# Renumbering the places of all pieces in a planned decoder layer, with own places for the first and the last batch

## The reference

```python
# part 1: attention against a fixed memory of 1024 rows, 4 heads of 64 channels
x = _layernorm(residual, ln_g, ln_b)
scores = jnp.einsum('bhtd,sd->bhts', q, k)
p = jnp.square(jax.nn.relu(scores))
out = jnp.einsum('bhts,sd->bhtd', p, v)          # residual + out
# part 2: cross attention, 16 heads of 16 channels
logits = jnp.einsum('bhqd,bhkd->bhqk', Q, K) * scale
D = jnp.clip(frac[:, None, :] - frac[:, :, None], CLAMP_MIN, CLAMP_MAX)
stoich_bias = ap * jnp.maximum(D, 0.0)[:, None] + an * jnp.minimum(D, 0.0)[:, None]
probs = jax.nn.softmax(gamma * logits + delta * stoich_bias, axis=-1)
# part 3: eight experts with a common matrix and a LoRA of rank 4 each; the gate's argmax picks one
lora = jnp.einsum('bsr,fr->bsf', jnp.einsum('bsd,rd->bsr', x, lora_A[i]), lora_B[i])
inter = jax.nn.relu(base + lora)
expert_out = jnp.einsum('bsf,df->bsd', inter, wo_W) + wo_b
# the layer
x = _layernorm(x + attn(x)); x = _layernorm(x + xattn(x, ctx)); x = _layernorm(x + ffn(x))
```

## Time and profile before

| | |
|---|---|
| median of 3 runs | 916.64 us (914.18 to 917.05) |
| profiled execution, device time | 914.81 us |
| its span in the profile | 913.0 us |
| mean granted PE clock | 0.992 of full speed |
| instructions | 20283 |
| PE busy | 857.1 us, 94% |
| DVE busy | 778.7 us, 85% |
| ACT busy | 690.3 us, 76% |
| POOL busy | 533.2 us, 58% |
| DMA | 46.10 MB, mean 50 GB/s |

### The profile page before, as it was taken

One profiled execution on the slowest core, in us unless ns is written; L12 is line 12 of the kernel. 1 busy time (PEld: TensorE's weight loads), 2 busy tenths in 40 slices (PEclk: granted clock), 3 DMA queues, 4 the chain that ended last, 5 costly groups with the idle time before them and its releaser, 6 DMA issues.

```text
span 913.0 us, 20283 instructions
## 1 busy us (share of the span) xinstructions
PE 857.1 (94%) x7140; PEld 682.6 (75%) x7140; DVE 778.7 (85%) x2286; ACT 690.3 (76%) x1453; POOL 533.2 (58%) x620
## 2 busy tenths in 40 slices
PE   2697989999999999999999999999999999999876
PEld 1344767878878787877887787887878787788666
DVE  3869989889998998989898998989899897899842
ACT  3557889788787878878787978878797887877721
POOL 2757776666656765666666666665666565533210
PEclk9989999999999999999999999999999999999998
DMA  5223322222122223122222322212222312223000
GB/s 151 87 46 68 65 47 54 36 54 41 35 48 58 54 48 64 35 44 55 39 54 58 54 44 53 45 32 51 59 54 47 64 33 32 58 38 66 14 13 23
DMA packets 40022, 46.10 MB, mean 50 GB/s; under 512 B 10257, under 2 KB 27153, under 8 KB 39922
## 3 DMA queue, kind: packets, MB, share of 16 engines
q1 hardware_dynamic: 39922, 44.82, 24.6%
HBM read 15.42 MB, written 4.19 MB: 21 GB/s over the span
## 4 chain that ended last, share of the span: by engine, by line
PE 83%; DVE 8%; ACT 3%; issue 2%; DMA 1%; POOL 1%; SPq 0%; POOLq 0%; DVEq 0%
PE bank L218 28%; PE bank L262 12%; PE bank L343 11%; PE bank L250 7%; PE bank L334 6%; PE bank L355 6%; PE bank L251 6%; PE bank L282 2%; PE bank L404 2%; DVE bank L761 2%; PE bank L365 1%; DVE T L768 1%; DVE R L717 1%; DMA STG<-in_WvT 1%; PE bank L239 1%
## 5 line engine op out<-in xcount | busy, mean ns | idle before, releaser
L964 POOL TENSOR_SCALAR U<-DP,alph 128x512 f32<-128x512 f32 x256 | 181.5, 711 | 153.6 <-DVE NM L768 92.3
L953 POOL TENSOR_TENSOR R<-R 128x512 f32<-128x512 f32 x212 | 221.9, 1052 | 78.4 <-ACT R L496 78.4
L548 ACT ACTIVATE P<-T,NM 128x256 f32<-128x256 f32 x512 | 232.0, 508 | 3.2 <-DVE NM L768 2.7
L761 DVE SCALAR_TENSOR_TENSOR bank<-DN,alph,bank 128x512 f32<-128x512 f32 x256 | 191.9, 750 | 36.7 <-PE bank L334 35.0
L475 ACT ACTIVATE STG<-bank 128x512 f32<-128x512 f32 x256 | 152.5, 596 | 70.5 <-PE bank L343 69.1
L768 DVE CUSTOM_DVE_ANT_0 T<-bank,U 128x256 f32<-128x256 f32 x512 | 197.0, 422 | 8.8
L496 ACT ACTIVATE R<-bank 128x512 f32<-128x512 f32 x256 | 151.8, 597 | 54.4 <-PE bank L251 53.3
L343 PE MATMUL bank<-ident,P 128*128 128x128 f32 x1024 | 154.6, 273 | 5.0 <-ACT STG L475 4.8
L343 PEld LDWEIGHTS bank<-ident,P 128*128 128x128 f32 x1024 | 119.3, 140 | 24.0 <-ACT P L548 8.4
L262 PE MATMUL bank<-R,VS 128*32 128x512 f32 x1024 | 124.5, 604 | 5.5 <-DVE R L717 5.2
L250 PE MATMUL bank<-SK,KH 128*128 128x512 f32 x256 | 114.9, 449 | 8.2 <-DVE SK L711 7.6
(11 more groups left out here) (165 smaller groups left out, 1863.3 us busy)
## 6 DMA issues: line engine op xcount, KB each, us to landing
QS<-QK SPq DMA_DIRECT2D x384, 64.0 KB, 2.3
XG<-in_x SPq DMA_DIRECT2D x16, 256.0 KB, 2.7
CT<-in_ctxT SPq DMA_DIRECT2D x16, 256.0 KB, 3.6
out<-XO SPq DMA_DIRECT2D x16, 256.0 KB, 2.2
FK<-in_frac SPq DMA_DIRECT2D x16, 128.0 KB, 3.5
STG<-in_wiT SPq DMA_DIRECT2D x2, 512.0 KB, 3.5
STG<-in_woT SPq DMA_DIRECT2D x2, 512.0 KB, 4.0
STG<-in_kT SPq DMA_DIRECT2D x2, 256.0 KB, 4.0
```

The source lines that it names most:

```text
L548: eng.activation(P[n % NP][:, cs], T[n % NT][:, cs], ACT.Exp, bias=NM[:, n % 8, q:q + 1], scale=-1.0).then_inc(s_ex, 1)
L761: eng.scalar_tensor_tensor(out=L[:, :], in0=dn[:, :], scalar=alph[:, 16 + h:17 + h], in1=L[:, :], op0=ALU.mult, op1=ALU.add).then_inc(s_t1, 1)
L953: eng.tensor_tensor(r[:, :], r[:, :], r[:, :], ALU.mult).then_inc(s_sqp, 1)
L964: eng.tensor_scalar(U[n % NU][:, :], dp[:, :], alph[:, h:h + 1], 0.0, ALU.mult, ALU.add).then_inc(s_u, 1)
```

## The change

Every piece stays, with the same instructions. `due` gets two more arguments: `early` is added to the place of batch 0, `late` to that of batch 15 (batches 1 to 14 keep the common place). Nearly every place gets a new number, and so do the places of the pieces that come once (the weights, the staged loads, the constants, the memsets). As places fix nothing but the order of a queue, what changes is that order: 161 of PE's 1313 pieces, 220 of ACT's 1083, 203 of DVE's 698, 210 of POOL's 584 and 85 of SP's 140 stand at another position of their queue.

```diff
-        def due(g, first, count=1, step=0, start=0):
+        def due(g, first, count=1, step=0, start=0, early=0, late=0):
             for u in range(count):
-                b, over = divmod(g - first - step * u, PERIOD)
-                if over == 0 and start <= b < NB:
+                at = g - first - step * u
+                if at == early and start == 0:
+                    yield 0, u
+                b, over = divmod(at, PERIOD)
+                if over == 0 and max(start, 1) <= b < NB - 1:
                     yield b, u
+                if at == PERIOD * (NB - 1) + late:
+                    yield NB - 1, u
...
@@ PE
-                for b, u in due(g, 1322, 4, 24):
+                for b, u in due(g, 1323, 4, 25, early=1, late=292):
                     ffn_in(b, u)
...
-                for b, u in due(g, -939, 4, 141):
+                for b, u in due(g, -939, 4, 141, early=34):
                     av(b, u)
...
-                for b, _ in due(g, 1265):
+                for b, _ in due(g, 1269, early=-4, late=255):
                     uT(b)
-                for b, u in due(g, -1159, 16, 37):
+                for b, u in due(g, -1159, 16, 37, early=8):
                     scores(b, u)
-                for b, _ in due(g, -1219):
+                for b, _ in due(g, -1226, early=-87, late=9):
                     xnT(b)
...
@@ ACT
-                if g == -740:
+                if g == -577:
                     weight("i0", WI[0][:, 0:1, :], view(1024, 0, 128, 1))
...
-                if g == -853:
+                if g == -718:
                     weight("p0", WP[0][:, 0:4, :], view(1024, 1, 128, 4))
-                if g == -847:
+                if g == -665:
                     weight("p1", WP[0][:, 4:8, :], view(1024, 2, 128, 4))
...
-                for b, _ in due(g, 1282):
+                for b, _ in due(g, 1269, early=-17, late=303):
                     ulh(b)
...
@@ DVE
-                for b, _ in due(g, 2):
+                for b, _ in due(g, 1, early=-11, late=8):
                     differences(b)
...
-                for b, u in due(g, 14, 16, 39):
+                for b, u in due(g, 12, 16, 39, early=2, late=-2):
                     biased(16 * b + u)
...
-                if g == -1944:
+                if g == -2010:
                     dve.wait_ge(d_x[0], 16)
                     stats("a", 0, XG[0])
-                for b, _ in due(g, -1422):
+                for b, _ in due(g, -1428, early=-272, late=-4):
                     dve.wait_ge(s_xnT, b)
                     centred("a", b, XN, XG[b % 2], s_x0)
-                if g == -1392:
+                if g == -1513:
                     first_gain()
-                for b, _ in due(g, -1499, start=1):
+                for b, _ in due(g, -1491, start=1, late=-3):
...
-                for b, _ in due(g, 866):
+                for b, _ in due(g, 885, early=-23, late=-8):
                     low("aoT", b, CL, CH, s_aoh, s_aol)
-                for b, _ in due(g, -1215):
+                for b, _ in due(g, -1218, early=-178):
                     skl(b)
...
-                for b, _ in due(g, 2064):
+                for b, _ in due(g, 2020, early=-28, late=338):
                     dve.wait_ge(d_o, 16 * b)
                     centred("d", b, XO, X2b, s_xo)
-                if g == -629:
+                if g == -825:
                     dve.wait_ge(d_small, 160)
                     eng.tensor_scalar(bqk[:, 0:2], bqk[:, 0:2], gd[:, 0:1], 0.25, ALU.mult, ALU.mult)
                     eng.tensor_scalar(alph[:, :], alph[:, :], gd[:, 1:2], None, ALU.mult).then_inc(s_small, 1)
-                if g == -1825:
+                if g == -1430:
                     weight("v", W["v"][1][:, :, :], view(512, 1, 128, 2), W["v"][0][:, :, :])
-                if g == -1328:
+                if g == -1203:
                     weight("k", W["k"][1][:, :, :], view(512, 2, 128, 2), W["k"][0][:, :, :])
...
-                if g == -528:
+                if g == -479:
                     weight("i0", WI[1][:, 0:1, :], view(1024, 0, 128, 1), WI[0][:, 0:1, :])
-                if g == -967:
+                if g == -859:
                     weight("i1", WI[1][:, 1:2, :], view(1024, 2, 128, 1), WI[0][:, 1:2, :])
-                if g == -642:
+                if g == -596:
                     weight("p0", WP[1][:, 0:4, :], view(1024, 1, 128, 4), WP[0][:, 0:4, :])
-                if g == -536:
+                if g == -482:
                     weight("p1", WP[1][:, 4:8, :], view(1024, 2, 128, 4), WP[0][:, 4:8, :])
-                if g == 74:
+                if g == -17:
                     weight("g", GA[1][:, :, :], view(80, 0, 128, 2), GA[0][:, :, :])
-                if g == -82:
+                if g == -191:
                     weight("lb", LB[64:96, :], stage(1024, 2)[64:96, :], LB[64:96, :])
...
-                for b, _ in due(g, 1278):
+                for b, _ in due(g, 1283, early=-15, late=249):
                     ull(b)
-                for b, u in due(g, -1147, 16, 39):
+                for b, u in due(g, -1140, 16, 38, early=24, late=-10):
                     if on_dve(b, u):
                         square(b, u)
...
@@ POOL
-                for b, _ in due(g, -1305, start=1):
+                for b, _ in due(g, -1326, start=1, late=4):
                     gain(b)
...
-                for b, u in due(g, -1085, 16, 36):
+                for b, u in due(g, -1087, 16, 36, early=36, late=7):
                     if not on_dve(b, u):
                         square(b, u)
...
@@ SP
-                for b, u in due(g, 78, 4, 119):
+                for b, u in due(g, 109, 4, 119, early=1, late=-121):
                     restack(4 * b + u)
-                for b, _ in due(g, 85, start=1):
+                for b, _ in due(g, -235, start=1, late=-196):
                     load_f(b)
```

More of the change, by code:

```diff
@@ L440, in _ @@
                     values(4 * b + u)
-                for b, _ in due(g, -410):
+                for b, _ in due(g, -428, early=17, late=-22):
                     otT(b)
-                for b, _ in due(g, 885):
+                for b, _ in due(g, 894, early=-5, late=5):
                     turned_over("aoT", b, AO, s_ao, 2 * b + 2, s_aoT)
-                for b, _ in due(g, 925):
+                for b, _ in due(g, 924, early=-4, late=-2):
                     op(b)
-                if g == -1022:
+                if g == -1051:
@@ L448, in _ @@
                     bias_o()
-                for b, _ in due(g, -262):
+                for b, _ in due(g, -262, early=9, late=9):
                     turned_over("x1T", b, X1, s_x1, 2 * b + 2, s_x1T)
-                for b, _ in due(g, -232):
+                for b, _ in due(g, -231, early=-12, late=-16):
                     kp(b)
-                for b, _ in due(g, -191):
+                for b, _ in due(g, -200, early=-20, late=-11):
                     qp(b)
-                for b, _ in due(g, -139):
+                for b, _ in due(g, -139, early=29, late=23):
@@ L592, in _ @@
             for g in GRID:
-                for b, u in due(g, 1331, 4, 24):
+                for b, u in due(g, 1329, 4, 28, early=-4, late=394):
                     ih(b, u)
-                for b, _ in due(g, -296):
+                for b, _ in due(g, -311, early=6, late=-23):
                     x1(b)
-                for b, u in due(g, 65, 16, 41):
+                for b, u in due(g, 68, 16, 41, early=-5, late=1):
                     exps(16 * b + u)
-                for b, _ in due(g, -1223):
+                for b, _ in due(g, -1227, early=-196):
@@ L600, in _ @@
                     skh(b)
-                for b, _ in due(g, -476):
+                for b, _ in due(g, -487, early=8, late=30):
                     heads_out(b)
-                for b, u in due(g, 131, 16, 40):
+                for b, u in due(g, 131, 16, 40, early=-2, late=2):
                     turned(16 * b + u)
-                for b, _ in due(g, 782):
+                for b, _ in due(g, 782, early=-24, late=63):
                     ov(b, 1)
-                for b, _ in due(g, 596):
+                for b, _ in due(g, 579, early=-3, late=-51):
@@ L608, in _ @@
                     ov(b, 0)
-                for b, _ in due(g, 909):
+                for b, _ in due(g, 906, early=2, late=125):
                     act.wait_ge(s_vp, min(b + 2, NB))
                     high("aoT", b, CH, s_aoT, s_aoh)
-                for b, _ in due(g, 1068):
+                for b, _ in due(g, 1057, early=8, late=20):
                     x2(b)
-                if g == -2083:
+                if g == -2397:
                     weight("v", W["v"][0][:, :, :], view(512, 1, 128, 2))
-                if g == -1670:
+                if g == -1580:
@@ L634, in _ @@
                     act.wait_ge(s_lbz, 1)
                     weight("lb", LB[0:96, :], stage(1024, 2)[0:96, :])
-                if g == -332:
+                if g == -318:
```

(20 more changed lines are left out.)

126 lines of the change are left out of this document (63 added, 63 removed).

## The result

| | median | runs | ratio to before (95%) |
|---|---|---|---|
| before | 916.59 us (914.18 to 917.20) | 12 | |
| changed | 919.11 us (917.41 to 921.36) | 12 | 1.0033 (1.0023 to 1.0043) |

The change makes the kernel slower. The ratio says 0.33%, about 3.0 us; the medians differ by 2.5. The prediction named 917.5 us as the likeliest time: 1.6 us too low, inside its range. The interval leaves out no change, but the bound of 0.3% that the prediction set lies within it, so the time is at the edge, on the side to which the forecast leaned (+0.9).

A forecast was written before the change was run, and what follows sets the result against it. PE, busy without a wait through ten steady periods of 52.30 us, was taken as the bound; +7.5 (steady) - 5.9 (front) - 0.7 (tail) = +0.9 on the median 916.64 gave 917.5 us, range 914.5 to 920.5 (909.5 to 922 with A and B).

The forecast's parts named there:

- Steady periods: DVE, eleven periods: `differences` ahead of `ull` makes PE's first `ffn_in` matmul later each time, +7.5 us in all.
- Rivals A and C: A: `ull` isn't late, 910.0 us, chance 0.18; C: POOL's `positive` comes between DVE's instructions each period, 925 us, chance 0.04.
- Front, first part: DVE, batch 0: `centred` no longer stands behind W_v's low half; first transpose 2.1 us sooner, at 12.8.
- Front, second part: Bqk and alph ahead of `centred` of batch 1, unlanded weights later: batch 1's first scores 4.3 us sooner, first transpose's 2.1 included.
- The clock: PE after the shorter idle stretch before batch 1's scores: full clock perhaps kept, `av` 1.9 or 3.6 us; half taken, 1.1 us.
- Front, third part: DVE: W_lb's low half and W_g earlier (+1.2, +0.2) against `differences` leaving its place (-1.4); -0.5 us taken.
- Tail: Last batches: a `biased` fills DVE's 0.52 us wait, `load_f` of batch 15 saves about 0.2; -0.7 us.
- Rival B: Front: DVE's contention with POOL leaves a gain of only 3.2 us, clock still falls; +4.3, 920.9 us, chance 0.20.
- Rival D: Whole kernel: new order nowhere on the deciding path, or losses have twins; 85% keep position; 916.6 us, chance 0.06.

The follow-up runs named there:

- Experiment 2: Kernel before with only `differences` put ahead of `ull` in batches 1 to 12: 923.54 us, ratio 1.0084.
- experiments 4 and 5: 4: experiment 1's kernel, POOL's memsets early, 911.52 us; 5: W_v's low half back ahead of `centred` there, 913.40; W_v alone behind `first_gain` in kernel before, 915.89 us.
- experiment 6: Experiment 1's kernel with bqk and alph put back to just before `skl` of batch 1: 915.46 us, ratio 0.9995.
- experiment 1: Changed kernel with `ull` put ahead of `differences` again, nothing else put back: 913.06 us, ratio 0.9980.
- experiment 8: Kernel before with four front edits: W_v behind `first_gain`, memsets early, bqk and alph ahead of `centred` of batch 1, W_p0/W_p1 behind relu11: 911.09 us, ratio 0.9963.
- the first kernel of experiment 9: Changed kernel with `ull` first and all of POOL's memsets, the second QS buffer's too, ahead of the first rsqrt: 911.28 us, ratio 0.9960.
- experiment 3: Unmodified repeats: changed kernel again, 920.00 us, ratio 1.0045; kernel before again, a single execution for a second trace, 916.68 us.

## Why the prediction came out as it did

- **Steady periods: right in mechanism and size.** Predicted 0.68 per period and 7.5 us in all; measured 0.63 and 6.9. The 1.41 of `differences`, the idle 0.42 before `ull`, the slack of 0.43 and the 0.06 from `ull`'s end to PE's start, all read from the trace of before, were the sum. Experiment 2 gives 0.67. In the changed kernel `differences` starts 0.08 before the end that the row of the last `biased` shows (417.44 against 417.52), where I had let it start after that end.
- **Rivals A and C fall.** `ull` is late in eleven of eleven periods (A), and no `positive` holds DVE up there: `differences` and `ull` take 1.85 us in a row from 417.44 to 419.29 (C). The Trainium skill's rule (SBUF — State Buffer, "Who interferes with whom") thus costs nothing at the place where I weighed it, and bites where I had not: see the next point.
- **Front, first part: 2.1 predicted, nothing that lasts measured.** This is the step that failed. The first transpose starts at 14.96 and 15.08 before, at 15.59 and 14.68 after. Counted from kT's low half, whose start differs between the traces, it is 7.75 and 7.22 before, 7.11 and 7.49 after: 0.6 sooner in the first pair, 0.3 later in the second. I moved `centred` to 10.42 and left its 0.73 us as they were, and did not look at what POOL does at that time. Its row for the factor ends at 10.38, and behind it in the queue stand two memsets of 0.95. `centred` beside them takes 2.21 or 2.60, and 0.73 without them (experiments 4 and 5). That is 1.5 to 1.9 of the 2.1.
- **Front, second part: 4.3 predicted with the 2.1 in it, 2.3 and 3.2 measured** in the two pairs of traces. The part proper, from the first transpose to batch 1's scores, fell from 30.16 and 29.93 to 27.21 and 27.10: 2.9 and 2.8 gained, where 4.3 - 2.1 = 2.2 was taken. The 1.35 of bqk and alph came in full (idle 2.83 for 4.18), and their duration fell from 2.98 to 0.46; experiment 6 confirms them with 2.1 us. What is missing is the first part.
- **The clock: 1.1 predicted, 0.5 to 1.4 measured, by luck.** From batch 1's scores to the first `otT` it took 6.38 and 5.74 us before, 5.00 and 5.25 after. But the clock was not kept: the `av` took 2.90 and 3.55 us, nearer to the 3.6 of the slow case than to 1.9. And with the same 2.83 us of idle time the same way took 6.20 in experiment 1, 6.41 in experiment 8 and 6.13 in the first kernel of experiment 9, with an `av` of 3.64 each time, as long as before the change. Besides, the low clock turns up in two more stretches, and differs from execution to execution of one kernel. The two traces of before differ by 1.9 us in their ends, and the stretches in which they part are those of the low clock (experiment 3). Of the 23 executions of before beside experiment 3, the ten with a mean granted clock of 0.988 or less took 915.95 us or more, the thirteen above it 914.2 to 916.2; that the clock makes the whole spread of 3 us is likely, not shown.
- **Front, third part: -0.5 predicted; +1.1 measured at the first logits, +0.5 to +0.6 at the first `biased`** (from the first `otT` to it 20.87 and 21.04 before, 21.47 and 21.49 after). W_lb's 1.22 us lies on the path to the first `restack`: PE waits 1.57 for QS. I had weighed it against `differences`, which leaves the place before the first `biased`; but that one is late only if the logits are in time, and they are not. And again I kept durations as they were. In their new places, beside POOL's `gain`, W_g and the first rows of `differences` took

```profile
64.66 1.33 DVE L671 TENSOR_TENSOR GAl<-STG,GAh 128x80 fp32r<-128x80 f32 x1
65.91 1.63 DVE L757 TENSOR_SCALAR DN<-FK,fT 128x256 f32<-128x256 f32 x2
```

  where before they took

```profile
76.89 0.24 DVE L665 TENSOR_TENSOR GAl<-STG,GAh 128x80 fp32r<-128x80 f32 x1
70.87 0.60 DVE L751 TENSOR_SCALAR DN<-FK,fT 128x256 f32<-128x256 f32 x2
```

- **Tail: -0.7 predicted, -0.3 measured.**
- **The total came near because the range was wide.** Forecast were a loss of 7.5 and gains of 6.6. The loss was 6.9; the gains were 2.0 in the first pair of traces and 3.7 in the second, a third and just over a half of that. The sum moved from +0.9 to some +3 and stayed inside the range.
- **Rival B has the better account.** A front that gives 3.4 + 0.3 against 6.9 makes +3.2 (1.7 + 0.3 makes +4.9), and the ratio says +3.0; B said +4.3. Its condition, a front under 4.7 with the steady loss whole, is met. B put the loss of the front on DVE's contention with POOL, right as a kind. Between 26 and 45 us it did cost something (`centred` of batch 1 took 2.25 in place of 1.46 and 1.79), but the scores came sooner all the same; the loss that counts lay at 11.
- **Rival D's support was miscounted.** By the counts given with the change, 879 of 3818 pieces stand at another position, so 77% keep theirs, not 85%. It decides nothing: D falls with the 6.9 us.

## What to carry to other kernels

When a queue is full on one engine and another engine waits for it with a few tenths of slack, a swap costs (length of the piece moved ahead) - (idle time it fills) - (slack), once per period; all three can be read from one edge of the old trace. Here that is 1.41 - 0.42 - (0.43 - 0.06) = 0.62, where the 0.06 is what passes between the one engine's end and the other's start; 0.63 and 0.67 were measured. When a piece is moved in time, its duration is not a constant: look at what the other engines do in its new place, POOL's memsets too. And compare more than one trace of each kernel before a difference of 2 us in 900 is explained. And before a winning order is taken over whole, try its pieces one by one: here one swap of two pieces took back more than all the others gave, and four edits to the old order did better than the whole new one.

## What the runs showed of the hardware

- A float32 tensor_scalar on DVE of 128x256, twice, takes 0.73 us alone and 2.21 to 2.60 beside two of POOL's memsets of 128x1024, which themselves keep their 0.95. Two small tensor_scalars of DVE, on 2 and on 32 columns, took 1.00 and 1.98 us beside POOL's squares, 0.22 and 0.24 away from them. A tensor_tensor of DVE in `first_gain`, at 13.66 in the trace of experiment 1, kept its 0.69 beside the memset of LB (13.46, 0.99); one on 80 columns took 1.33 in place of 0.24 beside POOL's `gain`, which reads XN.
- The Trainium skill (SBUF — State Buffer, "🔬 SBUF: two separate sides") has one port pair that one engine's operation takes for the whole instruction while the other's waits; VectorE wants it in a two-port mode, or with two SBUF inputs, the latter only against a GpSimd operation that reads SBUF. The traces agree: a memset reads nothing, and it holds up the tensor_scalar and not the tensor_tensor, while `gain` holds up the tensor_tensor. That the tensor_scalar runs in a two-port mode no row here shows.
- The granted clock of PE after a stretch of idle time is not a function of the kernel's order alone. The two traces of before show it in the windows of experiment 3. After one and the same 2.83 us of idle time before batch 1's scores, the `av` behind them took 2.90 us in the first trace of the changed kernel and 3.55 in its second:

```profile
43.92 2.90 PE L268 MATMUL bank<-R,VS 128*32 128x512 f32 x16
```
```profile
42.51 3.55 PE L268 MATMUL bank<-R,VS 128*32 128x512 f32 x16
```
